# Experts' products of a slot mixture on one core: one float32 pass against three passes over high and low parts

## The reference

```python
logits = einsum('bnd,esd->bnes', x, se)            # 16 experts x 64 slots
dispatch = softmax(logits, axis=1); combine = softmax(logits over all slots)
slots = einsum('bnd,bnes->besd', x, dispatch)
gate = gelu(einsum('besd,edf->besf', slots, Wg) + bg)
up   = einsum('besd,edf->besf', slots, Wu) + bu
eout = einsum('besf,efo->beso', gate * up, Wd) + bd
y    = einsum('bns,bso->bno', combine, eout)
```

## Time and profile before

| what | us |
|---|---|
| median of 3 runs | 2756.94 (2753.6 to 2758.2) |
| the profiled execution, its own time | 2755.84 |
| its span (first to last instruction) | 2753.9 |
| PE busy | 2589.1 (94%) |
| `experts`, first matmul to first matmul of `combine` | 2273.5 to 2445.2 |

### The profile page before, as it was taken

How to read it: one execution, slowest core, us unless ns; L and a number is a source line. 1 busy time by engine, 2 the same in 40 slices (tenths; PEclk the granted TensorE clock), 3 DMA queues, 4 the chain that set the end, 5 groups by cost and what they waited for, 6 DMA issues and landing times. The chain is left out here.

```text
span 2753.9 us, 47808 instructions
## 1 busy us (share of the span) xinstructions
PE 2589.1 (94%) x16291; PEld 1543.9 (56%) x16291; DVE 2078.8 (75%) x5010; ACT 1634.3 (59%) x3370; POOL 443.7 (16%) x611
## 2 busy tenths in 40 slices
PE   7866999999999999999999999989999999999999
PEld 4433444444444444444444444347878788889999
DVE  8966989899899889989988998738474522346665
ACT  4531777777777777777777777866364522122221
POOL 4533111111111111111111111124121100100000
PEclk9975999999999999999999999999999999999999
DMA  7983362133033123303303000025343345435554
GB/s 244 315 241 40 46 84 34 17 46 45 6 48 45 22 30 46 39 12 46 46 14 40 8 6 8 8 104 214 106 170 136 109 161 180 163 132 194 193 189 156
DMA packets 177641, 257.63 MB, mean 94 GB/s; under 512 B 48756, under 2 KB 126712, under 8 KB 175896
## 3 DMA queue, kind: packets, MB, share of 16 engines
q1 hardware_dynamic: 160824, 239.26, 34.2%
q10 hardware_dynamic: 16608, 15.73, 1.9%
HBM read 158.30 MB, written 95.45 MB: 92 GB/s over the span
## 5 line engine op out<-in xcount | busy, mean ns | idle before, releaser
L768 ACT ACTIVATE att_pr<-att_ring 128x512 f32<-128x512 f32 (+3 forms) x2560 | 1174.4, 548 | 398.7 <-PE att_ring L848 391.4
L815 DVE TENSOR_REDUCE att_mx<-att_ring 128x1 f32<-128x512 f32 x1536 | 968.0, 680 | 77.0 <-PE att_ring L861 73.9
L861 PE MATMUL att_ring<-att_ks,att_qs 48*128 48x512 f32 (+3 forms) x1920 | 647.7, 422 | 17.0 <-ACT att_pr L768 7.0
L848 PE MATMUL att_ring<-att_qs,att_ks 64*128 64x512 f32 (+3 forms) x1920 | 575.0, 406 | 9.8 <-DMA att_qs<-att_mrow 4.9
L848 PEld LDWEIGHTS att_ring<-att_qs,att_ks 64*128 64x128 f32 x1920 | 300.5, 186 | 406.2 <-DVE att_mx L815 143.4
L821 DVE CUSTOM_DVE_ANT_0 att_junk<-att_ring,w_causal 128x256 bf16<-128x256 f32 (+3 forms) x1024 | 466.0, 486 | 67.6 <-PE att_ring L861 42.2
L887 PE MATMUL att_acc<-att_pr,att_v 128*32 128x512 f32 (+3 forms) x3840 | 451.5, 542 | 2.7 <-ACT att_cT L779 1.5
L861 PEld LDWEIGHTS att_ring<-att_ks,att_qs 48*128 48x128 f32 x1920 | 307.4, 185 | 144.7 <-ACT att_pr L768 106.4
L726 POOL TENSOR_SCALAR_AFFINE_SELECT att_pr<-att_pr 128x512 f32<-128x512 f32 x256 | 163.1, 637 | 1049.5 <-ACT att_pr L768 1049.5
L861 PE MATMUL att_ring<-g_ks,g_qs 48*128 48x512 f32 (+3 forms) x640 | 225.5, 463 | 17.2 <-PEq L137 7.8
L1452 ACT CAST com_e1h<-com_tp 128x1024 fp32r<-128x1024 f32 x64 | 64.8, 1017 | 236.4 <-PE com_tp L1512 236.4
(11 more groups left out here) (162 smaller groups left out, 3225.1 us busy)
## 6 DMA issues: line engine op xcount, KB each, us to landing
slot_exps<-dis_e SPq DMA_DIRECT2D x64, 512.0 KB, 2.7
com_e<-slot_exps SPq DMA_DIRECT2D x64, 512.0 KB, 3.5
att_qs<-q_parts SPq DMA_DIRECT2D x72, 256.0 KB, 12.0
q_parts<-proj_part SPq DMA_DIRECT2D x32, 512.0 KB, 4.3
dis_y<-y_rows SPq DMA_DIRECT2D x32, 512.0 KB, 3.9
att_ks<-k_parts SPq DMA_DIRECT2D x72, 128.0 KB, 12.8
y_rows<-proj_y SPq DMA_DIRECT2D x16, 512.0 KB, 4.4
y_cols<-proj_yT SPq DMA_DIRECT2D x16, 512.0 KB, 5.3
```

The costliest lines, as they stand in the source:

```text
L768: nc.scalar.activation(pr[:, s % NPR, h, off:CH], spot(("s", s, h)), ACT.Exp, scale=float(HD) ** -0.5).then_inc(exp_done, 1)
L815: nc.vector.tensor_reduce(dst, spot(e), AX.X, ALU.max).then_inc(mb_used, 1)
L848: nc.tensor.matmul(spot(e), ks[g][r, kb * P:(kb + 1) * P], qs[g][r, c, hf * CH + off:(hf + 1) * CH], start=True, stop=True).then_inc(sT_re ...
L861: nc.tensor.matmul(spot(e), qs[g][r, c, q0:q0 + P], ks[g][r, j * CH:j * CH + wd], start=True, stop=True).then_inc(mb_ready, 1)
```

## The change

Gate, up and down products of experts 1 to 15 (down also of expert 0) are made from float32r parts in three matmuls each. `gate_up(0)` stays a float32 product. The parts are made by three engines: ACT rounds Wg, Wu, Wd and h (`gate_high`, `up_high`, `down_high`, `hidden_high`); DVE subtracts for Wu, Wd and h (`up_low`, `down_low`, `hidden_low`); POOL makes both parts of the slots and the low part of Wg (`slots_parts`, `gate_low`). The parts have two buffers each; the raw weights now have two buffers (`NR = 2`) in place of four, and a load waits for the subtraction that reads the buffer last. `gate` and `h` have fewer buffers. `output` of an expert moves one expert later on DVE. SP asks for the bias of expert e+2 at expert e, behind the loads of expert e+2, where it was that of e+4.

```diff
-    NB = 4
+    NR, NB = 2, 4
@@ sync
+                def load(e):
+                    if e < E:
+                        for dst, src, loaded, split, n in ((wg, "Wg", gate_in, wg_split, e - NR),
+                                                           (wu, "Wu", up_in, wu_split, e - NR),
+                                                           (wd, "Wd", down_in, wd_split, e - NR + 1)):
+                            if e >= NPRE + NR:
+                                sp.wait_ge(split, n)
+                            sp.dma_start(dst[:, e % NR], io[src][e]).then_inc(loaded[e % NR], 16)
                 for e in range(E):
                     if e >= NPRE:
-                        load_gu(e + NB)
-                    if e + NB < E:
-                        load_bias(e + NB)
-                    if e >= NPRE:
-                        load_down(e + NB)
+                        load(e + NR)
+                    if e >= 2:
+                        load_bias(e + NB - 2)
                     if e == E - NB:
                         com["load_first"](sp)
@@ scalar
+                gate_high(1)
+                up_high(1)
+                down_high(0)
                 for e in range(E):
+                    gelus(e, (0, 1))
+                    if 1 <= e < E - 1:
+                        gate_high(e + 1)
+                    hidden_high(e, (0, 1))
+                    if 1 <= e < E - 1:
+                        up_high(e + 1)
+                    gelus(e, (2, 3))
+                    if e >= 1:
+                        down_high(e)
+                    hidden_high(e, (2, 3))
                     if e >= 3 and e % 2:
                         round_pair((e - 3) // 2)
@@ vector
+                up_low(1)
+                down_low(0)
+                for e in range(E):
+                    hidden(e, (0, 1))
+                    if e >= 2:
+                        output(e - 2)
+                    hidden_low(e, (0, 1))
+                    if 1 <= e < E - 1:
+                        up_low(e + 1)
+                    hidden(e, (2, 3))
+                    if e >= 1:
+                        down_low(e)
+                    hidden_low(e, (2, 3))
+                output(E - 2)
                 output(E - 1)
@@ gpsimd
+                def slots_parts(e):
+                    ...
+                    nc.gpsimd.tensor_copy(part(slh), src).then_inc(sl_high, 1)
+                    pool.wait_ge(sl_high, e)
+                    nc.gpsimd.tensor_tensor(part(sll), src, part(slh).bitcast(F32), ALU.subtract).then_inc(sl_split, 1)
+                    pool.wait_ge(sl_split, e)
+                def gate_low(e):
+                    pool.wait_ge(wg_high, e)
+                    nc.gpsimd.tensor_tensor(wgl[:, e % 2], weights(e)[0], wgh[:, e % 2].bitcast(F32),
+                                            ALU.subtract).then_inc(wg_split, 1)
+                    pool.wait_ge(wg_split, e)
+                for e in range(1, E):
+                    slots_parts(e)
+                    gate_low(e)
+                    if e >= 5 and e % 2:
+                        pair_low((e - 5) // 2)
+                pair_low(SB - 2)
@@ tensor, gate_up
+                        pe.wait_ge(sl_split, e)
+                        pe.wait_ge(wg_split, e)
+                        pe.wait_ge(wu_split, e)
...
+                                    for lhs, rhs in ((hi, slh), (hi, sll), (lo, slh)):
+                                        last = nc.tensor.matmul(dst[:, f, :], lhs[:, e % 2, k, cols], rhs[:, e % 2, k, :],
@@ tensor, down
+                    pe.wait_ge(wd_split, e + 1)
+                    pe.wait_ge(hl_ready, FB * e + FB)
+                            for lhs, rhs in ((hh, wdh), (hh, wdl), (hl, wdh)):
```

More of the change, by code:

```diff
@@ L1259, in _ @@
                     load_bias(e)
[L1260 to L1262 removed]
+                for e in range(NPRE, NPRE + NR):
+                    load(e)
                 for e in range(E):
                     if e >= NPRE:
[L1265 to L1269 removed]
+                        load(e + NR)
+                    if e >= 2:
+                        load_bias(e + NB - 2)
@@ L1274, in _, with up_high, gate_high, down_high @@
             def _(act):
+                def up_high(e):
+                    wait_weights(act, e, up_in)
+                    if e >= 3:
+                        act.wait_ge(gu_ready, 2 * (e - 2) + 2)
+                    nc.scalar.copy(wuh[:, e % 2], weights(e)[1]).then_inc(wu_high, 1)
+                def gate_high(e):
+                    wait_weights(act, e, gate_in)
+                    if e >= 3:
+                        act.wait_ge(gu_ready, 2 * (e - 2) + 2)
+                    nc.scalar.copy(wgh[:, e % 2], weights(e)[0]).then_inc(wg_high, 1)
+                def down_high(e):
+                    wait_weights(act, e, down_in)
+                    if e >= 2:
+                        act.wait_ge(o_ready, e - 1)
+                    nc.scalar.copy(wdh[:, e % 2], weights(e)[2]).then_inc(wd_high, 1)
+                def gelus(e, fs):
+                    for f in fs:
+                        act.wait_ge(gu_ready, 2 * e + f // 2 + 1)
+                        if FB * e + f >= 2:
+                            act.wait_ge(h_ready, FB * e + f - 1)
+                        nc.scalar.activation(gate[:, f % 2, :], gp[:, f, :], ACT.Gelu,
+                                             bias=w["bgT"][:, f, e:e + 1]).then_inc(gate_ready, 1)
+                def hidden_high(e, fs):
+                    for f in fs:
+                        act.wait_ge(h_ready, FB * e + f + 1)
+                        if e >= 2:
+                            act.wait_ge(o_ready, e - 1)
+                        nc.scalar.copy(hh[:, e % 2, f, :], h[:, f, :]).then_inc(hh_ready, 1)
                 def round_pair(s):
@@ L1314, in output @@
                                                 ALU.add).then_inc(eo_ready, 1)
-                hidden(0)
-                for e in range(1, E):
-                    hidden(e)
-                    output(e - 1)
+                up_low(1)
+                down_low(0)
+                for e in range(E):
+                    hidden(e, (0, 1))
+                    if e >= 2:
+                        output(e - 2)
[3 more added lines that the diff above has]
+                    hidden(e, (2, 3))
+                    if e >= 1:
+                        down_low(e)
+                    hidden_low(e, (2, 3))
+                output(E - 2)
                 output(E - 1)
@@ L1327, in _, with pair_low @@
             def _(pool):
-                for s in range(SB - 1):
+                def slots_parts(e):
+                    src = pre["slots"][:, :, e // 2, e % 2]
+                    part = lambda t: t[:, e % 2].rearrange("p k (b j) -> p b k j", b=B)
+                    if e == 1:
+                        pool.wait_ge(pre["slots_in"], 16 * (B - 1))
+                    if e >= 3:
+                        pool.wait_ge(gu_ready, 2 * (e - 2) + 2)
+                    nc.gpsimd.tensor_copy(part(slh), src).then_inc(sl_high, 1)
[7 more added lines that the diff above has]
+                    pool.wait_ge(wg_split, e)
+                def pair_low(s):
                     pool.wait_ge(high_ready, s + 1)
@@ L1361, in down @@
                     for r in range(RB):
+                        rows = slice(r * P, (r + 1) * P)
                         for f in range(FB):
-                            last = nc.tensor.matmul(op[:, e % 2, r, :], h[:, e % 2, f, r * P:(r + 1) * P],
-                                                    weights(e)[2][:, f, :], start=(f == 0), stop=(f == FB - 1))
+                            for lhs, rhs in ((hh, wdh), (hh, wdl), (hl, wdh)):
+                                last = nc.tensor.matmul(op[:, e % 2, r, :], lhs[:, e % 2, f, rows], rhs[:, e % 2, f, :],
+                                                        start=(f == 0 and lhs is hh and rhs is wdh),
+                                                        stop=(f == FB - 1 and lhs is hl))
                     last.then_inc(o_ready, 1)
```

104 lines of the change are left out of this document (56 added, 48 removed).

## The result

The changed kernel takes 2791.0 us (median of 4 runs, 2787.1 to 2794.0), the kernel before 2755.9 (median of 4, 2753.6 to 2758.2): a ratio of 1.0127, 95% interval 1.0109 to 1.0144. It is slower by 35 us, beyond the upper end of the predicted range, 2783, and past rival D's 2778. The profiled execution took 2787.1 us, its span is 2785.2, 31.3 longer than before.

What follows compares the result with a forecast made beforehand. PE alone was taken to bound `experts`, busy 30.00 of 30.00 us. Start 11.9, beats 148.6, loads 3 and end 12.6 made 176.1 us against 167.4, 8.7 more: 2766 us, range 2741 to 2783.

Steps and rivals of the forecast that it cites:

- rival D: In experts, POOL gets in at each boundary or its slot work is slower: beats 11.0 and 12.1, 2778 us; chance 0.17.
- C's point of decision: Rival C: DVE and POOL hardly meet, 2737 us, chance 0.14; the change gains below a mean beat of 10.0 us.
- I take it that POOL gets in there.: In experts, POOL enters between hidden_low and up_low: eight beats of 9.8, six of 11.7, 148.6 us; chance 0.42.
- the clock, dismissed with 0.04: In experts, three passes do not shorten PE's work, needing a clock that falls in waits of 1 to 3 us; chance 0.04.
- The start: Before gate_up(1), POOL's second instruction waits 7.3 us behind a pool configuration: 11.9 us and not 8.54, 3.4 us lost.
- The loads: At expert 15, load_first's 3 MB ahead of Wg and Wu makes Wg(15) late: 3 us, bounds 0 and 5.
- PE's gain: In experts, three float32r passes take 8.61 us per expert against 10.36: 26.8 us saved if nobody makes PE wait.

Runs made afterwards that it cites:

- psum_in: Changed kernel, with DVE's subtractions for Wu, Wd and h taking their second input from a PSUM tile of zeros; 2740.0 us.
- hl_merged: Changed kernel, with the two DVE subtractions of h of a half done as one of 128x512; 2780.8 us.
- before_256: Kernel before, with the line 1066 subtractions of the dispatch stage in pieces of 256 columns in place of 512; 2762.4 us.
- warm16: Changed kernel, with 16 unused matmuls of constants ahead of each gate_up from expert 2 on; 2779.9 us, ratio 1.0097.
- cfg_early: Changed kernel, with one unused POOL addition of 128x8 behind the last all-reduce of dispatch; 2780.8 us.
- h_psum: Changed kernel, with h in PSUM and its rounding and subtraction done once per half; 2745.8 us, ratio 0.9975.
- h_psum_all: h_psum plus the small POOL addition of cfg_early and combine's first loads asked for at expert 13, not 12; 2733.9 us, ratio 0.9922.
- bias_early: Changed kernel, with the bias of e+4 asked for at expert e, where the change asks for e+2; 2885.7 us.
- first_late: Changed kernel, with the twelve first loads of combine at expert 13, behind the weights of expert 15; 2787.1 us.

## Why the prediction went wrong, and where it was right

**Direction and mechanism: right.** The kernel became slower because the new DVE and POOL work shares one interface, though no engine taken alone passes the beat: psum_in shows it, by 8.5 in place of 11.0 / 12.1 with one operand moved. C's point of decision, a mean beat of 10.0, holds too: all versions under it gained, and those over it lost. The size is wrong: 35 us slower where the forecast had 9.

**The step that failed: "I take it that POOL gets in there."** I let POOL in once, ahead of `up_low`, and not between the two `hidden_low`, on the strength of the run of line 1066 in the earlier trace rows. The changed kernel's timeline and hl_merged show it at both boundaries. That was rival D, priced at 11.0 and 12.1; measured 10.97 and 12.07. It is 160.2 us for 14 beats against my 148.6: 11.6 us. One run of one kind of instruction was the only evidence for "not between like instructions" (the same trace has a second one, at 1942.50, of the same kind), and I gave it more weight than the earlier trace rows, where POOL came in at the first boundary that it met. The rows had the difference in them that all kept traces show (under before_256): in the earlier trace rows POOL had held DVE up just before (1.76 us for 1.22), in the earlier trace rows it had not, and my own beat has `gate_low` hold up the first `hidden_low`.

**The second step that failed: the clock, dismissed with 0.04.** No term of the sum has it. I looked at `combine`, where 6.9 us of PE's waits in 284 leave the clock at 1.00. But the beat that I had worked out myself has PE idle at one place for over 1 us, and D's for 2.4 and 3.5, in every expert. The stretches at the low level cost 11.5 us in eight `gate_up`s and 2.7 in expert 15 (8.5 for 5.83). With D's order the new waits made their own surcharge, which has a price in none of my cases; that is what carries the result past D's 188.1, to 200.0. warm16 takes it out of experts 2 to 14.

**The sum.** Start 11.94, forecast 11.9. From `gate_up(1)` to `gate_up(15)` 172.5, forecast 151.6: 160.2 of beats, 11.5 of clock, 0.8 of loads. From there 15.5, forecast 12.6. In all 200.0 for 176.1, 23.9 more: 11.6 + 11.5 + 2.9 - 2.2, and rounding. The median of the runs lies 3.9 above the profiled execution, where I allowed 1.1; those other executions have no profile, so these 3 us stay open.

**The start: right.** 3.4 us by an instruction waiting 7.7 us behind its configuration (I took 7.3); cfg_early takes it away. By the figure of the Trainium skill, some 6 us (GPSIMD Engine Reference, "2.1 Instruction dispatch"), it would have been 2.0; the waits of this kind in the kept traces run from 6.6 to 8.9 us, those ahead of `experts` from 7.5 to 8.9.

**The loads: right in kind, size off.** 3 us forecast at expert 15, 0.8 in the changed kernel. I put that down to the longer beats, but PE's wait before `gate_up(15)` does not simply follow the beat: it was 4.1 in the changed kernel, 4.6 in psum_in, 7.3 in h_psum and 8.6 in hl_merged. That `load_first` makes it is shown by h_psum_all, where it is gone; what sets its size is not. An early bias costs much, as bias_early shows, whose beats (19.8 to 22.4) were longer still than its expectation had them (17 to 19).

**PE's gain: right.** Where nobody makes PE wait the beat is 8.5 (psum_in), I had 8.61.

**Left open.** Why POOL never comes in within a long run of line 1066 in `dispatch` but at each boundary in `experts`. Length, operation, a further wait and operands written in place are excluded. Nor is it who asked first, by the start times: in the earlier trace rows POOL asked at 2056.20, ahead of DVE's next start at 2056.53, and stayed out; in `experts` it asked at 2365.95, ahead of the second `hl` at 2366.09, and got in. That POOL gets in behind a DVE instruction that it held up, or behind the first of a sequence, and not into a run that goes on undisturbed, fits all cases, but was not tried by itself. That `first_late` helps the total by itself isn't shown either.

## What to carry to other kernels

When DVE gets instructions with both inputs in SBUF while POOL works, add the two engines' times for that work as if for one engine, price each boundary at which POOL can come in ahead of what PE waits for, and first look whether one operand can sit in PSUM: `h` there, with the pieces merged, turned a beat of 11.0 / 12.1 into 8.8. When a change opens a wait of some us on PE once per iteration, add the low-clock cost of the matmuls behind it (here some 1.45 us, in eight of 14 experts) before calling the wait small. Try the halves of such a change by themselves: both gained alone, one of them once its loads had buffers enough.

## What the runs showed of the hardware

- DVE's two-input instructions from SBUF and POOL's instructions exclude each other. In `experts`, ahead of `wul`, POOL came in at each DVE boundary where it was waiting, so a pair of `hl`, 0.75 us beside nothing, took 2.13 us in the timeline above, and `wul` 2.28 for 1.22. In `dispatch`, beside a long run of DVE instructions that POOL had not held up, a POOL instruction of 1.04 us took 4.5 to 5.9.
- Repeated waits of 2 to 3.3 us on PE were followed by a stretch at the lower clock in about half of the experts; a wait of 2.24 us was in one case and one of 3.15 us was not in another. 16 matmuls without use ahead of each `gate_up` from expert 2 on removed the stretches in experts 2 to 14 and made the stage 7.6 us shorter.
- The wait behind POOL's configuration was 6.6 to 8.9 us over all traces and belongs to the first subtraction or addition after an all-reduce; the rounding ahead of it (0.61 us) did not have to wait.
